# Turning the attention probabilities on VectorE and through memory instead of on TensorE

## The reference

```
x = x + tanh(g_xattn) * attention(layernorm(x), ctx, ctx)
x = x + tanh(g_ffn) * ffn(layernorm(x))

attention: 32 query heads, 8 key/value heads, head size 128, 64 keys per batch
  queries = rope(q @ Wq.T); keys = rope(k @ Wk.T); values = v @ Wv.T
  scores = queries . keys * 128**-0.5, causal mask over the 64 keys
  attn = softmax(scores);  out = (attn @ values) @ Wd.T
```

## Time and profile before

| | us |
|---|---|
| median of 3 runs | 1546.08 (1544.65 to 1546.61) |
| profiled execution | 1548.8 |
| its span, first to last instruction | 1547.0 |
| PE busy | 1480.5 (96%) |
| DVE busy | 990.7 (64%) |
| POOL busy | 624.5 (40%) |
| ACT busy | 537.4 (35%) |

### The profile page before, as it was taken

How to read it: one execution, slowest core, us unless ns; L and a number is a source line. 1 busy time by engine, 2 the same in 40 slices (tenths; PEclk the granted TensorE clock), 3 DMA queues, 4 the chain that set the end, 5 groups by cost and what they waited for, 6 DMA issues and landing times.

```text
span 1547.0 us, 19240 instructions
## 1 busy us (share of the span) xinstructions
PE 1480.5 (96%) x7488; PEld 1214.2 (78%) x7488; DVE 990.7 (64%) x1536; ACT 537.4 (35%) x829; POOL 624.5 (40%) x403
## 2 busy tenths in 40 slices
PE   7899999999999999999999999999999999968996
PEld 7878888888888888877778888888888888855553
DVE  4956565656565656565675656464656565678995
ACT  4424131414141413144341414141413132317883
POOL 2534243434343333330443434343333333225996
PEclk9999999999999999999999999999999999998998
DMA  8823131313222222217341313121212221193553
GB/s 275 251 59 101 36 97 28 93 40 78 54 75 56 76 56 68 64 58 251 89 138 32 87 28 83 35 77 42 75 43 73 45 59 32 44 287 108 188 177 136
DMA packets 193786, 142.92 MB, mean 92 GB/s; under 512 B 147744, under 2 KB 162592, under 8 KB 193312
## 3 DMA queue, kind: packets, MB, share of 16 engines
q1 hardware_dynamic: 193264, 138.54, 31.5%
q0 software_dynamic: 432, 3.15, 1.0%
HBM read 124.88 MB, written 19.92 MB: 94 GB/s over the span
## 4 chain that ended last, share of the span: by engine, by line
PE 82%; DVE 7%; ACT 3%; POOL 3%; DMA 2%; issue 1%; SPq 1%; POOLq 0%; ACTq 0%
PE psum L511 16%; PE psum L513 16%; PE psum L512 16%; PE psum L565 7%; PE psum L600 7%; PE psum L601 7%; PE psum L602 7%; POOL go L1180 2%; PE psum L574 2%; DVE stat L1252 1%; DVE sc L1551 1%; ACT xg L1050 1%; ACT xu L1051 1%; DVE xt_lo L1208 1%; ACT xi L1055 1%
## 5 line engine op out<-in xcount | busy, mean ns | idle before, releaser
L511 PE MATMUL psum<-xt_hi,wq_hi 128*128 128x512 f32 x1024 | 405.2, 396 | 2.0 <-DVE xt_lo L1208 2.0
L513 PE MATMUL psum<-xt_hi,wq_lo 128*128 128x512 f32 x1024 | 400.1, 391 | 0.0
L512 PE MATMUL psum<-xt_lo,wq_hi 128*128 128x512 f32 x1024 | 399.4, 390 | 0.0
L1112 POOL TENSOR_TENSOR rot<-rot 128x1024 f32<-128x1024 f32 x64 | 153.5, 2399 | 430.7 <-DVE rot L1312 429.0
L1360 DVE TENSOR_TENSOR acc<-psum,acc 128x512 f32<-128x512 f32 x256 | 175.8, 688 | 164.7 <-PE psum L602 162.6
L1084 POOL TENSOR_TENSOR wd_lo<-wd_raw,wd_hi 128x512 fp32r<-128x512 f32 x128 | 164.3, 1290 | 244.6 <-ACT wd_hi L857 244.6
L511 PEld LDWEIGHTS psum<-xt_hi,wq_hi 128*128 128x128 f32 x1024 | 192.9, 188 | 41.1 <-DVE xt_lo L1208 2.8
L513 PEld LDWEIGHTS psum<-xt_hi,wq_lo 128*128 128x128 f32 x1024 | 192.5, 188 | 40.8
L512 PEld LDWEIGHTS psum<-xt_lo,wq_hi 128*128 128x128 f32 x1024 | 193.0, 188 | 38.3
L893 ACT ACTIVATE vw_hi<-psum 64x512 fp32r<-64x512 f32 x256 | 151.3, 591 | 203.6 <-PE psum L513 200.4
L1084 POOL TENSOR_TENSOR wq_lo<-wq_raw,wq_hi 128x512 fp32r<-128x512 f32 x128 | 162.3, 1284 | 139.4 <-ACT wq_hi L852 139.4
(11 more groups left out here) (130 smaller groups left out, 1964.9 us busy)
## 6 DMA issues: line engine op xcount, KB each, us to landing
wq_raw<-in_wq_t SPq DMA_DIRECT2D x128, 256.0 KB, 4.5
wd_raw<-in_wd_t SPq DMA_DIRECT2D x128, 256.0 KB, 3.1
acc<-in_x SPq DMA_DIRECT2D x16, 512.0 KB, 5.4
x_scratch<-acc SPq DMA_DIRECT2D x16, 512.0 KB, 8.1
xa<-x_scratch SPq DMA_DIRECT2D x16, 512.0 KB, 3.3
xb<-x_scratch SPq DMA_DIRECT2D x16, 512.0 KB, 4.2
xn<-in_x SPq DMA_DIRECT2D x10, 512.0 KB, 4.7
wk_raw<-in_wk_t SPq DMA_DIRECT2D x4, 1024.0 KB, 8.1
```

The source lines that it names most:

```text
L511: pe.matmul(dst, a_hi, b_hi, start=start, stop=False)
L512: pe.matmul(dst, a_hi, b_lo, start=False, stop=False)
L513: return pe.matmul(dst, a_lo, b_hi, start=False, stop=stop)
L1112: pool.tensor_tensor(rot[:, 0, :, :], rot[:, 0, :, :], rot[:, 1, :, :], ALU.add).then_inc(rope_done, 1)
```

## The change

60 of the 64 units have their probabilities turned in another way; the last two units of each half (30 and 31 of 32) keep the PE transposes. For the others:

- DVE transposes `prob` in place, in blocks of 32x32 (at the end of `softmax_b`).
- SP stores the tile to memory (`p_scratch`, 128 rows of 2 KB), waits until it has landed, waits until the previous unit's low part is done, and loads it back with four DMAs, one per block of 32 keys, each to 32 partitions in pieces of 32 values (`move_probs`). The tile that is loaded is `pt_raw`, in SBUF.
- ACT's copy and DVE's subtraction read `pt_raw` instead of `p_turned`. DVE's subtraction of the maximum for the next unit waits for the store instead of PE's transposes, before it writes `prob`.

Orders change too: on PE the output blocks 0 and 1 of a group come later in the slot of kind 0 and block 2 moves to the slot of kind 1; on ACT `copy_probs` goes behind the query weights in kinds 1 and 2, and in kind 0 it and the exponential go ahead of `values` 7 and the query weights; on DVE `lower_probs` moves later within each slot and the first additions go behind `softmax_b`; on SP one Wd load goes behind the new move.

```diff
+            def move_probs(unit):
+                n = moves(unit)
+                sp.wait_ge(turned_done, n)
+                sp.dma_start(p_dram[n % 2, :, :, :, :, :].rearrange("a q t c i -> (a q) (t c i)"),
+                             prob[:, :, :].rearrange("p s k -> p (s k)")).then_inc(p_out, 16)
+                sp.wait_ge(p_out, 16 * n)
+                if unit:
+                    sp.wait_ge(pt_lo_done, unit)
+                for c in range(4):
+                    sp.dma_start(pt_raw[32 * c:32 * c + 32, :, :, :],
+                                 p_dram[n % 2, :, :, :, c, :].rearrange("a q t i -> q t a i")).then_inc(pt_in[n % 2], 16)
...
@@ SP, slot
                     if u % UPG == 3:
-                        for i in range(2, 6):
+                        for i in range(2, 5):
                             next_wd(VPG * gg + i)
+                    if u >= 1 and moved(unit - 1):
+                        move_probs(unit - 1)
+                    if u % UPG == 3:
+                        next_wd(VPG * gg + 5)
...
@@ PE, slot
                 queries(unit, 0)
                 if kind == 0:
-                    if filled:
-                        turn_probs(unit - 2)
                     queries(unit, 1)
                     if filled:
                         values(gg - 1, 6)
                     queries(unit, 2)
-                    if filled:
-                        outputs(gg - 1, 0)
...
                     queries(unit, 5)
+                    if filled:
+                        outputs(gg - 1, 0)
                     queries(unit, 6)
                     if filled:
-                        outputs(gg - 1, 2)
+                        outputs(gg - 1, 1)
...
                 if kind == 1:
                     if filled:
-                        turn_probs(unit - 2)
+                        outputs(gg - 1, 2)
                         outputs(gg - 1, 3)
...
                 if kind == 2:
-                    turn_probs(unit - 2)
...
@@ ACT, slot
                 if kind == 0 and filled:
-                    copy_probs(unit - 2)
                     copy_values(gg - 1, 6)
                     split_wd(VPG * gg - 1)
+                    copy_probs(unit - 2)
+                    exponential(unit - 1)
+                    copy_values(gg - 1, 7)
                     next_wq(unit, 0)
                     next_wq(unit, 1)
                     split_wd(VPG * gg)
-                    copy_values(gg - 1, 7)
-                    exponential(unit - 1)
...
@@ DVE, softmax_a and softmax_b
-                if unit:
-                    dve.wait_ge(pt_ps, unit)
+                if unit and moved(unit - 1):
+                    dve.wait_ge(p_out, 16 * moves(unit - 1))
+                elif unit:
+                    dve.wait_ge(pt_ps, turns(unit - 1))
...
+                if moved(unit):
+                    blocks = prob[:, :, :].rearrange("p s (m k) -> p s m k", k=32)
+                    dve.wait_ge(p_done, unit + 1)
+                    dve.transpose(blocks, blocks).then_inc(turned_done, 1)
...
@@ DVE, slot
                 if kind == 0:
                     if filled:
                         turn_second(unit - 1)
+                        lower_values(gg - 1, 6)
                         lower_probs(unit - 2)
-                        lower_values(gg - 1, 6)
-                        add(gg - 1, 0)
                         softmax_a(unit - 1)
                         lower_values(gg - 1, 7)
...
                         softmax_b(unit - 1)
+                        add(gg - 1, 0)
                         add(gg - 1, 1)
-                        add(gg - 1, 2)
...
@@ DVE, slot, kind 3
+                    softmax_a(unit - 1)
                     lower_probs(unit - 2)
-                    softmax_a(unit - 1)
                     turn_first(unit)
```

More of the change, by code:

```diff
@@ L163, in gated_block @@
             acc = sb(s, "acc", [HTILES, DIM], F32)
-            kv_b = sb(s, "kv_b", [2 * KVC], F32)
+            with ExitStack() as over:
+                kv_b = sb(over, "kv_b", [2 * KVC], F32)
+            pt_raw = sb(s, "pt_raw", [BT, 4, 32], F32)
         with ExitStack() as s:
@@ L284, in kv_bank, with moved, moves, turns @@
             return bank(S_BANK + b % 2)
+        def moved(unit):
+            return unit % UNITS < UNITS - 2
+        def moves(unit):
+            return unit + 1 - 2 * (unit // UNITS)
+        def turns(unit):
+            return unit % UNITS - (UNITS - 2) + 1 + 2 * (unit // UNITS)
         def there(n):
@@ L570, in turn_probs @@
                 pe.wait_ge(p_done, unit + 1)
-                if unit:
+                if turns(unit) > 1:
                     pe.wait_ge(pt_lo_done, unit)
@@ L614, in slot @@
                     queries(unit, 2)
-                    if filled:
-                        outputs(gg - 1, 0)
-                    else:
+                    if not filled:
                         turn_rows(half, 4)
@@ L625, in slot @@
                     queries(unit, 4)
+                    if not filled:
+                        turn_rows(half, 6)
+                    queries(unit, 5)
+                    if filled:
+                        outputs(gg - 1, 0)
+                    queries(unit, 6)
                     if filled:
                         outputs(gg - 1, 1)
[L628 to L632, removed]
-                        outputs(gg - 1, 2)
                     else:
@@ L878, in copy_probs @@
                 p, b, gg = (unit // HB) % 2, unit % HB, unit // UPG
-                act.wait_ge(pt_ps, unit + 1)
                 if gg >= 1:
                     act.wait_ge(o_ps, (gg - 1) * OPG + (b + 1) * 2 * BT)
-                act.activation(pt_hi[:, p, b, :], p_turned, ACT.Copy).then_inc(pt_hi_done, 1)
+                if moved(unit):
+                    act.wait_ge(pt_in[moves(unit) % 2], 64 * ((moves(unit) + 1) // 2))
+                    src = pt_raw[:, :, :, :].rearrange("p t a i -> p (t a i)")
+                else:
+                    act.wait_ge(pt_ps, turns(unit))
+                    src = p_turned
+                act.activation(pt_hi[:, p, b, :], src, ACT.Copy).then_inc(pt_hi_done, 1)
             def copy_values(gg, i):
@@ L923, in slot @@
                 if kind == 1:
+                    next_wq(unit, 2)
+                    next_wq(unit, 3)
                     if filled:
                         copy_probs(unit - 2)
-                    next_wq(unit, 2)
-                    next_wq(unit, 3)
                     if unit > 1:
@@ L1343, in lower_probs @@
                 dve.wait_ge(pt_hi_done, unit + 1)
-                lower(pt_lo[:, p, b, :], p_turned, pt_hi[:, p, b, :], pt_lo_done)
+                src = pt_raw[:, :, :, :].rearrange("p t a i -> p (t a i)") if moved(unit) else p_turned
+                lower(pt_lo[:, p, b, :], src, pt_hi[:, p, b, :], pt_lo_done)
             def lower_values(gg, i):
@@ L1391, in slot @@
                     if filled:
-                        lower_probs(unit - 2)
+                        add(gg - 1, 2)
                         add(gg - 1, 3)
@@ L1397, in slot @@
                     if filled:
+                        lower_probs(unit - 2)
                         add(gg - 1, 5)
```

7 lines of the change are left out of this document (4 added, 3 removed).

## The result

The changed kernel takes 1554.26 us (median of 8 runs, 1549.29 to 1561.17) against 1545.92 for the kernel before on the same chip: a ratio of 1.0056, 95% interval 1.0041 to 1.0072. It is 0.6% slower, and the forecast was 1.3% faster. The profiled execution took 1556.32 us (span 1554.5).

A forecast was written before the change was run, and what follows sets the result against it. PE instructions times their pitch were taken to bound the attention stages. The profiled 1548.8 us, less 26.7 for removed turns, plus 7 of waits gave 1529.1, or 1526.4 against the median; range 1519 to 1547.

The forecast's parts named there:

- 60 turns at 0.445: On PE, each of the 60 removed turns (four transposes) gives back 0.445 us, 26.7 us gained.
- Rival D: On PE, removal gives back the full 272 ns of each transpose, 65 us, for 1488 us; chance 0.01.
- The transpose on DVE: 60 transposes of 128x512 f32 on DVE take 0.65 to 0.69 us each, 41 us more work, hidden as a sum.
- rival C: The DVE transpose takes two passes, 1.21 us, which adds 15 us, for 1542 us; chance 0.12.
- Term (c): ACT and DVE read the turned tile from SBUF instead of PSUM in the same time, 0.1 us each way.
- Steps 1 and 2: With T0 the start of the kind-0 slot, the turned tile is ready at T0 + 1.0 and landed at T0 + 8.4.
- rival B: The landing in kind 0 decides: gain gone at T0 + 9.8, up to 1567 us; chance 0.13 beyond break-even.
- Step 3: In the kind-0 slot, the chain from the tile's landing to the first addition takes 10.1 us.
- Step 4: In kind 0, landing may come by T0 + 7.9; at 8.4 PE stands 0.5 us, 14 times, 7 us lost.
- Step 5: In kind 0, POOL's sum for the scores ends at T0 + 6.0, wanted at T0 + 6.14: just in time, nothing added.
- I cost all of this at nothing: Outside the tight kind-0 chain, work queued later on SP, ACT and POOL (query weights, Wd block, value splits) has cover: no cost.
- rival E: The edits costed at nothing aren't free: one wait of 1.2 us a group leaves nothing gained, 1546 us; chance 0.07.

The follow-up runs named there:

- experiment 1: The kernel before without the 60 PE turns, ACT and DVE reading a constant tile instead (attention result not computed): 1519.27 us, ratio 0.9837.
- experiment 4: The changed kernel with the first two query-weight splits (ACT's copy, POOL's subtraction) moved from kind 0 to the start of kind 1: 1532.62 us, ratio 0.992.
- experiment 2: The changed kernel's orders on all engines, but every unit turned on PE and nothing sent through memory: 1547.63 us, ratio 1.0016 to the kernel before.
- experiment 3: The changed kernel with all its DMAs, but ACT and DVE read a constant tile without waiting for the loads (attention result not computed): 1530.57 us, ratio 0.9909.
- experiment 10: The kernel before with one wait added: in kind 0 POOL's first query-weight subtraction waits for the softmax's sum: 1546.22 us, ratio 1.0004.

## Why the prediction was wrong, step by step

- **60 turns at 0.445: right.** 26.7 forecast, 25.8 measured (experiment 1); the clean groups last 77.92 us there and 77.97 in experiment 4, 78.1 forecast. Rival D is out.
- **The transpose on DVE: right.** 712 ns against 650 to 690; rival C (1.21) is out. The 1.24 us that four times the figure of the Trainium skill, "VectorE: DVE Perf Modes", The three transpose paths, would give isn't what the trace has.
- **Term (c), the lowering from SBUF instead of PSUM "taken as the same time": wrong.** It isn't slower by itself (0.69), but it can now be held. From PSUM it took 0.69 us in 16 cases beside a POOL subtraction (experiment 2); from `pt_raw`, in SBUF, the 10 that started beside one took 0.76 to 1.77.
- **Steps 1 and 2, landing at T0 + 8.4: right in size, in part by luck.** In 13 of the 14 slots the copy starts at T0 + 7.5 to 8.9. Where the lowering of kind 3 took 0.69 us it starts at 7.5 to 8.0: the store and the loads take 0.5 less than forecast (6.5 to 7.2 from the end of the transpose to the copy in 13 slots, against 7.4). Where it was held, by about 0.7, it starts at 8.3 to 8.9. In the first filled slot of the second half it starts at T0 + 10.7, beyond rival B's 9.8, and PE stands 2.5 us there; that is one slot of fourteen, behind a late first group, so B isn't what made the kernel slower.
- **Step 3, "from landing to the first addition 10.1 us": the step that failed.** It took the multiply at 0.69 us and the scaling at 0.23; the multiply took 1.68 to 1.83 in 12 of 14 slots, the scaling 0.52 to 1.29 in 10 of them. In the example the chain lasts from 888.65 to the end of the first of two additions, about 899.9: 11.3. In the two slots with no stretch it lasts 10.2, as forecast, and in the twelve 11.2 to 12.3. (Two of its small terms were read 0.05 and 0.03 high: 892.82 to 893.46 is 0.64, and 886.41 to the end of the multiply is 1.90.) I had seen that POOL's splits go to T0 + 14 and POOL is free then, and costed their own lateness. I didn't ask what they would run beside. ACT's copies for them came at T0 + 14.2 to 17.1, in all 14 slots when the weights had landed. By my own sum the multiply was due at 8.4 + 10.1 - 0.74 - 0.65 - 0.69 = T0 + 16.4; POOL's two subtractions run from T0 + 16.6 to 19.6.
- **Step 4, "14 x 0.5 = 7 us lost": mis-sized by that.** The waits are 0.7 to 2.5 us, 15.8 us in 12 waits, and each costs PE about 0.3 more than its own length: the matmul before the wait at 899.99 starts at 898.84, so start to start it is 0.92 over the pitch where 0.76 is shown, and the next two starts are 0.12 late. The other additions' waits show the same 0.28 to 0.30. An estimate from these rows: with a chain of 10.2 everywhere, 11 of the 12 waits would be gone and the one behind the landing at 10.7 would be about 1.2. Step 4's own break-even of T0 + 7.9 fits: with the multiply at 0.69 (experiment 4) eleven slots landed by T0 + 8.0, the other three (8.2 to 8.9) were themselves made longer by a wait for scores, and none waited for addition 0. So even the 7 us were too many.
- **Step 5, the scores "just in time": right for the groups in which the lowering took 0.69.** Where a POOL subtraction meets the kind-3 lowering (1.4 to 1.8 us, ahead of 8 of the 14 slots), scores wait 0.5 to 1.2.
- **"I cost all of this at nothing": wrong, rival E in part.** In the first group of each half nothing is filled yet, slots are shorter, and the cover isn't there. Query weights are issued at 106.20 instead of 103.27, their copies on ACT start at 113.60 instead of 109.96, the exponential behind them at 115.18 instead of 112.78 though its input was ready at 110.4, and PE stands 3.17 us for the Wd block. In the second half waits of 3.00 and 3.40 for scores stand at this place; the kernel before had 1.77 and 2.59 there, and the orders alone (experiment 2) 1.77 and 3.26, so not all of it is the move's. Experiment 4, which has no stretched multiply, stands 13.3 above experiment 1, and that is the price of the first groups with what they leave behind.

The account: 1545.1 - 25.8 (turns) + 13.3 (first groups and what they leave behind) + 21.6 (DVE operations held by POOL's subtraction behind the late landing) = 1554.2; measured 1554.3. Its terms are differences between runs, so it closes by construction, and it joins chips (on the changed kernel's own chip the rise is 8.3). What carries it are the traces. From the changed kernel to experiment 4 the 12 waits for addition 0 go, the waits for scores in the groups fall from 5.8 to 1.4 us, and those at the start of the second half don't. Over the two attention stages PE waits 41.0 us in 32 waits in the changed kernel and 22.4 in 16 in experiment 4: 18.6 less, and 4.5 for sixteen restarts at 0.28, if all cost what those for additions do. The two profiled spans are 25.1 apart.

The 13.3 between experiments 1 and 4 (12.5 between the profiled spans) divide by the starts of the scores into 3.5 in the first half's first group, 0.7 in the rest of that half, 4.4 in the crossing (the orders alone bring 1.3 there) and 3.7 in the second half, with 0.4 behind; the held lowerings of the second half's later groups are in it. How much of that each cause takes was not measured apart.

## What to carry to other kernels

When an order change frees a piece of work on one engine to run later, look up what runs on the other engines at its new time, VectorE and GpSimd above all: being off the critical path doesn't keep it from stretching an operation that is on it. When a change moves an operand from PSUM to SBUF, ask the same of the operation that reads it: here its time alone stayed at 0.69 us, and what changed is what can hold it. Cost a pipeline's first round by itself, since the slack that hides a new wait in the filled rounds isn't there, and the lateness with which it ends may be passed on to the rounds behind it. When a remedy removes a wait, see in the trace whether something else left with it (experiment 3), before calling its gain the wait's price.

## What the runs showed of the hardware

- A DVE operation with both operands in SBUF stands while a POOL subtraction runs: multiply 0.69 to 1.74 us, a 128x8 scaling 0.23 to 1.13 (experiment 10). With one operand in PSUM it isn't held: two additions 1.28 (one alone 0.69; neighbours overlap), the lowering 0.69 in 16 cases (experiment 2). The same lowering with both in SBUF: up to 1.77.
- A 32x32 block transpose of 128x512 f32 on DVE takes 712 ns, as long as a multiply over that tile.
- Regrouping 256 KB through memory in pieces of 128 bytes: 2.0 us for the store, and four loads of 64 KB, issued in 2.6, have landed 4.8 us after the first issue (883.84 to 888.65 in the changed kernel).
- Four PE transposes between dense matmuls cost 0.43 us by the medians (25.8 / 60) and 0.48 by the clean groups ((79.85 - 77.92) / 4), though the profile gives each 272 ns.
- A wait of PE costs 0.28 to 0.30 us more than the idle time that the profile shows for it (13 waits for additions in the changed kernel).
